# Layer norm statistics taken tile by tile, three Newton steps instead of four, and scale and shift fused, in a four-layer graph network on one core

## The reference, cut to what matters

```
xn = layernorm(x);  x = x + graph_part(xn) + attention_part(xn)
x = x + ffn_part(layernorm(x))

layernorm(x) = (x - mean(x)) / sqrt(var(x) + 1e-5)          # over the 512 features
```

```
h = residual + agg(h) @ Wl.T + bl + h @ Wr.T
h = prelu((h - mu) * rsqrt(var + 1e-5) * g + b, a);  residual = h
```

## Time and profile before

| | |
|---|---|
| device time, three runs | 4931.12, 4932.30, 4932.89 us, median 4932.3 |
| the profiled execution's own time | 4929.59 us |
| its span | 4927.6 us |
| PE busy, DVE busy, ACT busy | 79%, 50%, 29% of the span |
| DVE instructions | 10718 |
| mean granted clock of TensorE | 0.962 |

### The profile page before, as it was taken

One profiled execution on the slowest core, in us unless ns is written; L12 is line 12 of the kernel. 1 busy time (PEld: TensorE's weight loads), 2 busy tenths in 40 slices (PEclk: granted clock), 3 DMA queues, 4 the chain that ended last, 5 costly groups with the idle time before them and its releaser, 6 DMA issues.

```text
span 4927.6 us, 161288 instructions
## 1 busy us (share of the span) xinstructions
PE 3898.6 (79%) x68148; PEld 2504.9 (51%) x68148; DVE 2478.6 (50%) x10718; ACT 1414.7 (29%) x4675; POOL 345.7 (7%) x314
## 2 busy tenths in 40 slices
PE   9878896877777666777777666666679996789998
PEld 7444453555555444555555444444446744545554
DVE  6323216477767555667776556665542535221111
ACT  0010111344444222444444222245531401011111
POOL 0000000000000222000000221012210000100000
PEclk9888998999999999999999999999999998889999
DMA  2000101200000000000000000000003301011111
GB/s 68 26 30 27 41 26 69 103 27 0 0 0 0 1 1 4 1 0 0 0 0 0 1 2 4 0 1 1 1 24 84 73 30 58 34 37 60 60 60 36
DMA packets 46351, 122.19 MB, mean 25 GB/s; under 512 B 24956, under 2 KB 32915, under 8 KB 35657
## 3 DMA queue, kind: packets, MB, share of 16 engines
q1 hardware_dynamic: 36490, 99.00, 5.9%
q0 software_dynamic: 9776, 22.00, 2.3%
HBM read 105.79 MB, written 14.92 MB: 24 GB/s over the span
## 4 chain that ended last, share of the span: by engine, by line
PE 62%; DVE 28%; issue 5%; ACT 4%; POOL 0%; DVEq 0%; ACTq 0%; POOLq 0%
PE PS L655 31%; PE PS L929 25%; DVE ls_turn L1796 11%; DVE ls_act L1801 4%; ACT ls_gate L1258 3%; PE PS L741 2%; DVE ls_pr L1805 2%; DVE ls_parts L1829 2%; DVE ls_parts L1824 1%; DVE ls_parts L1818 1%; PE PS L1026 1%; PE PS L686 1%; PE PS L1076 1%; DVE stats L1432 1%; PE PS L1016 1%
## 5 line engine op out<-in xcount | busy, mean ns | idle before, releaser
L929 PE MATMUL PS<-BUF,ls_parts 128*3 128x256 bf16 x60000 | 1856.8, 273 | 743.6 <-DVE ls_parts L1829 720.1
L929 PEld LDWEIGHTS PS<-BUF,ls_parts 128*3 128x3 bf16 x60000 | 1318.7, 84 | 1279.7 <-DVE ls_parts L1829 1107.1
L1796 DVE STREAM_TRANSPOSE ls_turn<-PS 128x256 f32<-128x256 f32 x1250 | 557.3, 446 | 488.5 <-PE PS L929 466.2
L655 PE MATMUL PS<-ring,BUF 128*125 128x512 f32 (+1 forms) x1440 | 617.8, 588 | 27.6 <-DVE BUF L1569 11.2
L655 PE MATMUL PS<-BUF,ring 128*128 128x512 f32 (+1 forms) x2176 | 594.6, 435 | 2.3 <-ACT BUF L1166 1.4
L1258 ACT ACTIVATE ls_gate<-ls_act 128x8 f32<-128x8 f32 x1250 | 261.6, 209 | 973.8 <-DVE ls_act L1801 970.5
L655 PEld LDWEIGHTS PS<-BUF,ring 128*128 128x128 f32 x2176 | 330.7, 191 | 273.1 <-issue 271.2
L655 PEld LDWEIGHTS PS<-ring,BUF 128*125 128x125 f32 x1440 | 270.5, 190 | 356.8 <-issue 333.2
L1262 ACT ACTIVATE ls_th<-ls_gate 128x2 f32<-128x2 f32 x1250 | 253.8, 203 | 454.9 <-DVE ls_gate L1810 454.9
L1174 ACT ACTIVATE BUF<-PS,cols 128x625 f32<-128x625 f32 x146 | 114.0, 782 | 712.8 <-PE PS L655 709.9
L1805 DVE SCALAR_TENSOR_TENSOR ls_pr<-ls_gate 128x4 f32<-128x4 f32 x1250 | 203.1, 162 | 178.1 <-ACT ls_gate L1258 173.5
(11 more groups left out here) (291 smaller groups left out, 3038.3 us busy)
## 6 DMA issues: line engine op xcount, KB each, us to landing
cell_bias<-BUF SPq DMA_DIRECT2D x5, 2441.4 KB
BUF<-cell_bias POOLq DMA_DIRECT2D x5, 2441.4 KB, 14.9
ring<-in_L_wo SPq DMA_DIRECT2D x11, 1024.0 KB, 4.8
ring<-in_L_wi SPq DMA_DIRECT2D x8, 1024.0 KB, 4.8
ring<-in_L_wg SPq DMA_DIRECT2D x8, 1024.0 KB, 4.8
ring<-in_L_wout SPq DMA_DIRECT2D x8, 1024.0 KB, 4.8
ring<-in_L_w SPq DMA_DIRECT2D x4, 1024.0 KB, 4.8
ring<-in_L_gnn_Wl SPq DMA_DIRECT2D x3, 1024.0 KB, 7.0
```

The source lines that it names most:

```text
L655: ins = nc.tensor.matmul(out, a, b, start=(j == 0), stop=(j == len(terms) - 1))
L929: ins = nc.tensor.matmul(ls_sum[f][32 * q:32 * q + 3, :].rearrange("p (j n) -> p j n", j=4), ls_cut[:, c, 1:6:2], ls_half[:, s, q, c, :, f ...
L1796: V.transpose(ls_turn[:, 8 * f:8 * f + 8, 1:33], ls_sum[f].rearrange("p (g n) -> p g n", g=8)).then_inc(ls_turned[f], 1)
```

## The change: what it does

normalize loses its statistics. A new function measure(src, t) takes them for one tile: statistics, a wait, aggregate. It is called wherever a tile that a norm will read has just been finished, and DVE waits for that tile's last write before it. For the first norm, and for the one after layer 3's attention, it is called in a loop over the five tiles ahead of the norm. add_out has a new argument last_term: with False it takes no statistics (three of its six stages). rsqrt does three Newton steps. In conv and in layer 3's attention the passes over all tiles become a chain per tile: (u - m) * g in one SCALAR_TENSOR_TENSOR, (that * r) + b in another. Layer 3's addition of beta to x moves ahead of the wait for L3.out.

```diff
-                for k in range(4):
+                for k in range(3):
...
-            def normalize(src, put):
-
-                for t in range(NT):
-                    st.done(V.bn_stats(stats[0:R, t, :], src[:, t, :]))
-                st.after()
-                for t in range(NT):
-                    st.done(V.bn_aggr(mv[0:R, t, :], stats[0:R, t, :]))
+            def measure(src, t):
+
+                st.done(V.bn_stats(stats[0:R, t, :], src[:, t, :]))
+                st.after()
+                st.done(V.bn_aggr(mv[0:R, t, :], stats[0:R, t, :]))
+
+            def normalize(put):
+
                 st.after()
...
             dve.wait_ge(x_in, 16)
+            for t in range(NT):
+                measure(Xr, t)
             norm_x("L0")
...
             def conv(i):
                 stage = f"L0.conv{i}"
+                if i:
+                    dve.wait_ge(*made(f"L0.h{i - 1}"))
                 for t in range(NT):
                     dve.wait_ge(*full(stage, t))
                     took(V.tensor_tensor(u5[:, t, :], bank(stage, t)[0:R, :], row(f"L0_gnn_bl{i}"), ALU.add), stage, t)
-                if i:
-                    dve.wait_ge(*evacd(stage))
-                    dve.wait_ge(*made(f"L0.h{i - 1}"))
-                    for t in range(NT):
+                    dve.wait_ge(*evacd(stage, t))
+                    if i:
                         st.done(V.tensor_tensor(u5[:, t, :], u5[:, t, :], hR[:, t, :], ALU.add))
-                    st.after()
-                dve.wait_ge(*evacd(stage))
+                        st.after()
+                    measure(u5, t)
...
                 def put(t, m, r):
...
+                    u = u5[:, t, :]
+                    st.done(V.scalar_tensor_tensor(u, u, m, row(f"L0_gnn_g{i}"), ALU.subtract, ALU.mult))
+                    st.after()
+                    st.done(V.scalar_tensor_tensor(u, u, r, row(f"L0_gnn_b{i}"), ALU.mult, ALU.add))
+                    st.after()
+                    st.done(V.tensor_scalar(hR[:, t, :], u, 0.0, slope, ALU.min, ALU.mult))
+                    st.after()
+                    ins = V.scalar_tensor_tensor(hR[:, t, :], u, 0.0, hR[:, t, :], ALU.max, ALU.add)
                     if i < 2:
                         make(ins, f"L0.h{i}")
                     else:
                         st.done(ins)
-                if i == 2:
-                    st.after()
-                    for t in range(NT):
+                        st.after()
                         st.done(V.tensor_tensor(Xr[:, t, :], Xr[:, t, :], hR[:, t, :], ALU.add))
-                    st.after()
+                normalize(put)
+                st.after()
...
                     if done:
                         make(ins, done)
+                        dve.wait_ge(*made(done, t + 1))
                     else:
                         st.done(ins)
+                        st.after()
+                    if last_term:
+                        measure(Xr, t)
...
                     took(V.tensor_tensor(Xr[:, t, :], bank("F1.y", t)[0:R, :], Xr[:, t, :], ALU.add), "F1.y", t)
+                    dve.wait_ge(*evacd("F1.y", t))
+                    measure(Xr, t)
...
-                dve.wait_ge(*evacd("L1f.hs"))
+                    dve.wait_ge(*evacd("L1f.hs", t))
+                    measure(Xr, t)
...
+                            if (j, e) == (1, 3):
+                                dve.wait_ge(*evacd(stage, i))
+                                measure(Xr, t)
...
                 for t in range(NT):
+                    st.done(V.tensor_tensor(Xr[:, t, :], Xr[:, t, :], row("L3_mix_beta"), ALU.add))
+                for t in range(NT):
                     dve.wait_ge(*full("L3.out", t))
...
-                st.after()
+                    st.after()
+                    measure(u5, t)
...
+                    u = u5[:, t, :]
+                    st.done(V.scalar_tensor_tensor(u, u, m, row("L3_mix_gamma"), ALU.subtract, ALU.mult))
+                    st.after()
+                    make(V.scalar_tensor_tensor(Xr[:, t, :], u, r, Xr[:, t, :], ALU.mult, ALU.add), "L3.done")
+                normalize(put3)
+                for t in range(NT):
+                    dve.wait_ge(*made("L3.done", t + 1))
+                    measure(Xr, t)
```

More of the change, by code:

```diff
@@ L1503, in conv, with put @@
                     took(V.tensor_tensor(u5[:, t, :], bank(stage, t)[0:R, :], row(f"L0_gnn_bl{i}"), ALU.add), stage, t)
-                if i:
-                    dve.wait_ge(*evacd(stage))
-                    dve.wait_ge(*made(f"L0.h{i - 1}"))
-                    for t in range(NT):
+                    dve.wait_ge(*evacd(stage, t))
+                    if i:
                         st.done(V.tensor_tensor(u5[:, t, :], u5[:, t, :], hR[:, t, :], ALU.add))
-                    st.after()
-                dve.wait_ge(*evacd(stage))
-                def put(t, m, r):
-                    st.done(V.tensor_scalar(u5[:, t, :], u5[:, t, :], m, r, ALU.subtract, ALU.mult))
-                normalize(u5, put)
-                st.after()
-                for t in range(NT):
-                    st.done(V.tensor_tensor(u5[:, t, :], u5[:, t, :], row(f"L0_gnn_g{i}"), ALU.mult))
-                st.after()
-                for t in range(NT):
-                    st.done(V.tensor_tensor(u5[:, t, :], u5[:, t, :], row(f"L0_gnn_b{i}"), ALU.add))
-                st.after()
-                slope = cols[0:R, COL_AT["a_prelu"]:COL_AT["a_prelu"] + 1]
-                for t in range(NT):
-                    st.done(V.tensor_scalar(hR[:, t, :], u5[:, t, :], 0.0, slope, ALU.min, ALU.mult))
-                st.after()
-                for t in range(NT):
-                    ins = V.scalar_tensor_tensor(hR[:, t, :], u5[:, t, :], 0.0, hR[:, t, :], ALU.max, ALU.add)
+                        st.after()
+                    measure(u5, t)
+                slope = cols[0:R, COL_AT["a_prelu"]:COL_AT["a_prelu"] + 1]
+                def put(t, m, r):
+                    u = u5[:, t, :]
+                    st.done(V.scalar_tensor_tensor(u, u, m, row(f"L0_gnn_g{i}"), ALU.subtract, ALU.mult))
+                    st.after()
+                    st.done(V.scalar_tensor_tensor(u, u, r, row(f"L0_gnn_b{i}"), ALU.mult, ALU.add))
[3 more added lines that the diff above has]
+                    ins = V.scalar_tensor_tensor(hR[:, t, :], u, 0.0, hR[:, t, :], ALU.max, ALU.add)
                     if i < 2:
@@ L1563, in attention, with add_out @@
                                          den[0:R, t, :].unsqueeze(2).to_broadcast([R, H, 64]), ALU.mult), L + ".num", t)
-            def add_out(stage, bias, done):
+            def add_out(stage, bias, done, last_term=True):
                 for t in range(NT):
@@ L1969, in _ @@
                 attention("L2", ALU.add, 1e-6)
-                add_out("L2.out", row("L2_mix_b_proj"), None)
+                add_out("L2.out", row("L2_mix_b_proj"), None, False)
                 def biased(i):
@@ L2015, in _ @@
                 dve.wait_ge(*made("L2f.prob"))
-                add_out("L2f.s2", row("L2_ffn_sb2"), None)
+                add_out("L2f.s2", row("L2_ffn_sb2"), None, False)
                 for j in range(2):
@@ L2098, in _ @@
                     make(V.tensor_tensor(og[:, t, :], og[:, t, :], row("L3_gnn_bias_g", 256), ALU.add), "L3.og")
-                add_out("L3.gout", row("L3_gnn_b3"), None)
+                add_out("L3.gout", row("L3_gnn_b3"), None, False)
                 for stage, dst, bias in (("L3.k", kR, "L3_mix_bk"), ("L3.v", vR, "L3_mix_bv")):
```

14 lines of the change are left out of this document (1 added, 13 removed).

## The result

| | before | changed |
|---|---|---|
| median of six runs | 4932.58 us | 4910.89 us |
| from, to | 4931.12, 4933.21 | 4909.44, 4911.45 |
| profiled execution | 4929.59 | 4909.44 |
| its span | 4927.6 | 4907.7 |
| DVE instructions | 10718 | 10662 |

The ratio is 0.9956, 95% interval 0.9943 to 0.9969: 21.7 us faster. The forecast was 31.5, and the time lies 1.9 above the end of the range. The two traces hold the same 4675 ScalarE instructions in the same order, so each one's start can be compared.

What follows compares the result with a forecast made beforehand. Dense products and the recurrence's products hold over half the chain, with norms on the path, not hidden. Newton steps 6.6, fusions 5.1 and hidden statistics 19.8 sum to 31.5 us, giving 4901; range 4890 to 4909.

Steps and rivals of the forecast that it cites:

- first norm: Norm at the kernel's start: statistics in a loop of their own, one Newton step less; 0.13 us saved.
- conv(1): Layer 0 convolution: hidden statistics and a shorter norm save 5.70 us, chains in place of passes 0.4; sum 6.1.
- conv(2), L0.out, norm: Layer 0's end: 5.70 us at the convolution's norm, 0.1 from chains, 1.5 at L0.out and its norm; sum 7.3.
- F1.y, L1.out, L2.gout: Three norms whose statistics hide between arriving tiles, all but the last tile's; 3.29 us saved at each, 9.87 together.
- L1f.hs: Norm after the recurrence: tiles come almost at once, nothing hides the statistics and their overlap is lost; 0.3 us lost.
- L2f.eo1: Norm whose tiles come 0.856 us apart, bound by PE; 0.4 us saved.
- layer 3 and last norm: Layer 3's attention: 3.29 us at its norm, 4.56 in the passes, 0.13 at the last norm; sum 8.0.
- Rival 1: Chains cost no more than passes, so some 10 us more gain: 4891; chance 3%.
- rival 2: Hiding fails because statistics delay evacuations; only eleven norms' Newton steps count, 6.6 us: 4926; chance 6%.
- Rival 3: The untouched 625-round recurrence gets slower; at 0.08 us a round it costs 50 and the kernel ends at 4951; chance 4%.
- GpSimd's queue only for layer 3's rows: At L2f.eo1, POOL's load of layer 3's rows comes 2.9 us later; put at 0, at most 2.9 if all exposed.
- TensorE's clock: Transposes after F1.y and L2.gout: shorter idle may leave the clock up; 0 to 3.8 us more gain, outside the sum.

Runs made afterwards that it cites:

- e1: Kernel before with three Newton steps in place of four and nothing else; 4936.99 us beside 4931.70, ratio 1.0010.
- e2: Changed kernel with four Newton steps and the separate passes of before in the convolutions and layer 3; 4928.95 us beside 4931.70, ratio 0.9989.
- e3: Kernel before with only the fused chains per tile in the convolutions and layer 3; 4928.11 us beside 4931.70, ratio 0.9991.
- e4: Changed kernel with GpSimd's memset of duo moved ahead of the load of the second half of rows; 4906.93 us, ratio 0.9948.
- e10: Changed kernel with 9 to 38 filling products in TensorE's idle times, which ended late; 4942.32 us beside 4931.65, ratio 1.0022.
- the filled pair: Kernel before and changed kernel, each with filling products cut to fit TensorE's idle times; 4930.30 and 4894.47 us beside 4928.38.
- e14: Changed kernel with 4 to 18 filling products cut to fit TensorE's idle times; 4894.47 us beside 4928.38, ratio 0.9927.
- e11: Changed kernel with early memset, fused instructions in passes over tiles, and batched statistics at three norms; 4901.92 us beside 4931.65, ratio 0.9937.
- e15: Changed kernel with early memset, fused passes and batched statistics, plus filling products cut to fit TensorE's idle times; 4894.64 us, ratio 0.9926.
- e13: Kernel before with 7 to 25 filling products cut to fit nine TensorE idle times; 4930.30 us beside 4928.38, ratio 1.0001.
- e5: Kernel before with three Newton steps and 21 small dependent VectorE instructions in layer 1's idle time; 4923.22 us beside 4928.47, ratio 0.9991.

## Why the prediction was right or wrong

The balance is made on the two profiled executions, whose spans differ by 19.9.

| place | forecast | shift |
|---|---|---|
| first norm | 0.13 | 0.5 |
| conv(1) | 6.1 | 6.2 |
| conv(2), L0.out, norm | 7.3 | 5.6 |
| F1.y, L1.out, L2.gout | 9.9 | 3.15 + 3.3 + 3.1 = 9.6 |
| L1f.hs | -0.3 | -0.5 |
| L2f.eo1 | 0.4 | 0.3 |
| layer 3 and last norm | 8.0 | 7.7 |
| all of these | 31.5 | 29.4 |
| recurrence | 0 | -1.4 |
| other stages, untouched | 0 | -8.1 |

**Right.** Statistics hide where the tiles come 3.4 to 6.9 apart; the prices of 0.60 a Newton step, 0.78 a fused link and 0.72 a dependent pass came within 0.02; the loss after the recurrence came (0.5 for 0.3). Rival 1 fell by 0.79 against 0.66, rival 2 by the shifts at the norms. Rival 3 did not strike here (1.4 us over 625 rounds, 0.002 each, inside the 2 us that the prediction allowed), but e1 shows that it was a real case: one of fifteen experiments lost 14.4 us in the recurrence, and four more, e2, e3, e4 and e10, between 2.6 and 5.0.

**Mis-sized.** conv(2) with L0.out lacks 1.7. Of it 1.15 is the memset: I named GpSimd's queue only for layer 3's rows. Its memset starts when x is finished, and before it ran beside the statistics, which the change takes away from there; the small instructions took their place.

**Failed.** The step is "TensorE's clock ... I leave it out of the sum ...: 0 to 3.8 more". It was given one sign, that of a gain, on the ground that shorter idle leaves the clock up, and only the transposes right behind two norms were looked at. It was a loss of about 8: 2.4 at the router behind L0f, 1.5 in F1's hidden products, 2.5 net in layer 1 up to its last norm, 3.2 from the last router on, and gains and losses of 1 to 2 beside them that come to a gain of 1.4. Not even the transposes after F1.y gained: 4.40 against 3.83 with 3.1 us less idle. The granted clock fell with them. In F1's products (494.5 to 553 us before, 483.1 to 543.1 changed) it is 0.90 and then 0.88. For layer 1's products up to L1.mk and for the last stage the views are these, each before and then changed (of the 3.3 us that the first pair shows, 1.7 comes back behind it); e4, with the same norms, is back at 0.93 in the last stage:

```profile
607.00:677.10 70.10, 68.25 (x233) 36.02 (x232) 12.82 (x30) 7.29 (x12) 0.00 (x0) 1.00 0.12 45
```
```profile
594.40:667.80 73.40, 71.55 (x233) 38.58 (x232) 13.93 (x33) 7.29 (x12) 0.00 (x0) 0.95 0.11 43
```

```profile
4870.00:4927.60 57.60, 41.23 (x108) 18.58 (x106) 10.18 (x11) 3.74 (x3) 0.00 (x0) 0.93 0.06 22
```
```profile
4850.00:4907.70 57.70, 41.32 (x96) 18.00 (x94) 10.18 (x11) 3.49 (x3) 0.00 (x0) 0.85 0.06 22
```

That the clock is the cause of the missing 8 us can be read from the two traces as a whole. Laid over the records of the granted clock, PE's records are at 1.2 GHz for 187.1 us before and for 201.1 in the changed kernel, although that clock lasts less long in all, 357.2 in place of 372.3 us: less of it falls on idle time, more on work. If work at half the clock takes twice as long, 14.0 us more of it cost 7 of the 8.1 (an estimate). The mean clock of the table above, 0.962 and 0.964, hides this. In the filled pair the same count is 180.7 and 170.3. For the router e4 shows it by an experiment. Open is by what rule a stage gets one granted clock or the other (the idle time just ahead of it is not enough, by layer 3's router), and why layer 2's stage changes between executions of one kernel.

## What to carry to other kernels

Sum a change on VectorE by its rows, and then give the TensorE stages behind every idle time that it alters a term of either sign, as large as the gap between their durations at the two clocks; here it came to 8 us against 31. Where TensorE must wait, harmless products in the idle time can pay: by medians they gave 12.2 us on the changed kernel (e14), 4.0 on e11 (e15) and -1.9 on the kernel before (e13), and they need their length read from a row of that very shape. Compare parts of a change by the shift of the same instructions in two traces, not by their totals: three parts gave 1.1 us singly and 21.7 together, and most of the difference lay in a loop that none of them touches.

## What had not been expected of the hardware

- An untouched loop took 4.473 us a round over 90 rounds in e1, which has fewer instructions ahead of it, and 4.349 in e5, which has 21 idle ones more. They ran on different chips, so the cause is not isolated.
- A VectorE instruction on 125x5 elements took 1.32 us instead of 0.17 beside a GpSimd memset of 0.93 us, in seven kernels of seven; statistics over 125x512 beside it kept their 0.68 in six of six.
- Forty router products, the same instructions, took 5.01, 5.85, 6.36 and 8.56 us (e13, e14, before, changed) at mean granted clocks of 0.89, 0.75, 0.69 and 0.50.
- Behind the same 19.4 us of idle, the same stage ran at 0.50 in one kernel and at 0.65 in another (changed and e4, layer 3).
